# Causal masks of a fused attention kernel: two matmuls into PSUM, or additions by VectorE in place

## The chip, the cores and the metric

The kernel runs on one core of one Trainium2 chip. A core has TensorE (PE in the profile: matmuls; PEld is its weight load), VectorE (DVE), ScalarE (ACT), GpSimd (POOL) and SyncE (SP), each with its own in-order queue, which wait for each other by semaphores. The metric is the device time of one execution in microseconds (us), smaller is better. Three runs of the kernel before took 1605.15 to 1606.68 us, median 1605.58.

## The reference, cut to what matters

Two layers stand one behind the other. The first is a causal attention with 2 x 16 = 32 (batch, head) pairs, 1024 tokens, head width 64, and a two-step graph network that reuses the attention weights; the second is a local attention with a feed-forward network and isn't touched by the change.

```
b, n, _ = x.shape                       # 2, 1024
q = (xn @ Wq) ... * scale ; k = (xn @ Wk) ... ; v = (xn @ Wv) ...
sim = jnp.einsum('bhid,bhjd->bhij', q, k)
mask_value = -jnp.finfo(sim.dtype).max
causal_mask = jnp.triu(jnp.ones((n, n), dtype=bool), k=1)
sim = jnp.where(causal_mask, mask_value, sim)
attn = jax.nn.softmax(sim.astype(jnp.float32), axis=-1)
out = jnp.einsum('bhij,bhjd->bhid', attn, v)
adj = jnp.clip(attn + eye, 0.0, 1.0); deg = jnp.sum(adj, axis=-1, keepdims=True)
feats = v
for l in range(2):
    h = feats @ gnn_w[l] + gnn_b[l]
    h = jnp.einsum('bij,bjd->bid', adj, h) / deg
    feats = gelu(h + feats)
out = out + feats @ lin_w + lin_b
```

## The kernel before, in words

The first part is a loop over t, the 32 pairs of batch and head, in which the stages of neighbouring heads are interleaved: while head t computes its scores, head t+1 computes its row maxima and head t-1 ends its graph steps. Nothing is scheduled automatically. Each engine's order is the order of the calls in its own function (`tensor`, `vector`, the ScalarE function, `gpsimd`, `sync`), written out by hand, and named signals (`p_` counted by PE, `d_` by VectorE, `a_` by ScalarE, `w_` by GpSimd) carry the dependences.

The scores are computed twice. `smax(t, k)` (12 units a head, PSUM banks 0 and 1 in turn, L613) makes a block of 128 queries by up to 512 keys, and VectorE reduces it to row maxima (L1520). `mrow` (L624) transposes the maxima, ScalarE copies them (L1067), and a DMA (L448) lays them down as a 65th row, so that `scores(t, k)` (12 tiles a head, banks 2 and 3 in turn, L641 and L642) gives scores with the maximum already subtracted, keys on the partitions. ScalarE takes two exponentials of each tile (L1077 to a plain fp32 tile `Es`, L1078 to the rounded `Eh`), VectorE takes out the diagonal (L1534, for the tiles on it) and the rounding rest `El` (L1537). `av` (L659 to L661) multiplies by the values, `graph1` (L680), `graph2` (L694, L695, closed by L699) and `graph2b` (L708) are the graph steps, `tailT` and `tail` (L720, L729) the output projection, `proj` and `projv` (L572 to L574, L593 to L595) make queries, keys and values of later heads. ScalarE's `feats` (L1093, L1096) needs another function table than the exponential, so each head has a table load ahead of it and one (1.28 us) ahead of the next head's first exponential.

Of the 12 units and of the 12 tiles 8 each lie on the diagonal. There a third matmul adds the mask: a bf16 identity times a bf16 mask of 128 x 128 (`cmB`, L615 and L644), in the same accumulation group.

A PE matmul that writes bank b waits until the reader of its last content is through: `smax(t, k)` for `d_max` of unit k-2, `scores(t, k)` for `a_eh` of tile k-2. In loops 18 to 29 VectorE also runs `onward` (layer normalization of finished rows, statistics L1448 to L1461 with one step on GpSimd, L1316), in loops 2 to 5 a smaller `normed`; both stand behind `smax(t+1, 5)`.

Of the kernel before, what the change touches and what calls it, by code (L numbers as in the profile page):

```python
# [77 lines left out]
def program(nc, I, OUT):  # L78
    with ExitStack() as ctx:
# [51 lines left out]
        cmB = sb1([P, 2, P], BF16)  # L131
# [102 lines left out]
        maxes = [(t, k) for t in heads for k in (range(NTL) if t == 0 else (0, 1, 2, 3, 4, 5, 6, 7, 8, 9, 11, 10))]  # L234
        hops = [(t, k) for t in heads for k in (0, 2, 1, 3, 4, 5, 7, 9, 6, 8, 10, 11)]
# [39 lines left out]
        d_ident = signal("d_ident", ["R", "B", "cm"])  # L275
# [4 lines left out]
        d_max = signal("d_max", maxes)  # L280
        d_nm = signal("d_nm", heads)
# [234 lines left out]
        def tensor(e):  # L516
# [81 lines left out]
            def smax(t, k):  # L598
# [5 lines left out]
                q.wait_ge(*d_ident["cm"])  # L604
# [21 lines left out]
            def scores(t, k):  # L626
# [118 lines left out]
            for t in range(NH + 2):  # L745
                scores(t, 0)
                if t in (6, 7):
                    turn(t - 4, 6)
                graph2(t - 1, 9)
                scores(t, 1)  # L750
                graph2(t - 1, 6)
                scores(t, 2)
                smax(t + 1, 0)
                smax(t + 1, 1)
                scores(t, 3)
                tailT(t - 2, 0)
# [19 lines left out]
                projv(t + 1, 0)
                projv(t + 1, 1)
                graph2(t - 1, 8)
                scores(t, 6)
                av(t, 2)  # L780
                smax(t + 1, 6)
                scores(t, 7)
                graph2(t - 1, 10)
                smax(t + 1, 7)
                av(t, 3)
                scores(t, 8)
                smax(t + 1, 8)
                av(t, 4)
                smax(t + 1, 9)
# [228 lines left out]
        def scalar(e):  # L1018
# [50 lines left out]
            def scores(t, k):  # L1069
# [4 lines left out]
                q.wait_ge(*p_sc[t, k])  # L1074
# [62 lines left out]
            for t in range(NH + 2):  # L1137
                scores(t, 0)
                if t in (6, 7):
                    turn(t - 4)  # L1140
                scores(t, 1)
                scores(t, 2)
                scores(t, 3)
                if t == 0:
                    linear(1, 6)
# [6 lines left out]
                if t == 0:  # L1152
                    linear(3, 6)
# [768 lines left out]
```

## Time and profile before

| | |
|---|---|
| median of 3 runs | 1605.58 us (1605.15 to 1606.68) |
| the profiled execution, own time | 1606.24 us |
| its span | 1604.5 us |
| PE busy | 1444.8 us, 90% |
| VectorE busy | 1187.4 us, 74% |
| ScalarE busy | 995.6 us, 62% |
| GpSimd busy | 370.2 us, 23% |

Busy time is the time in which at least one instruction of the engine is recorded. A matmul's record includes the time until its last result is in PSUM, in which the next one already streams, so consecutive records of PE overlap; the distance between two starts is what a matmul costs the stream. The same holds, to a smaller degree, for VectorE and ScalarE. "[0.26 <-ACT t L1078]" behind a row means 0.26 us idle ahead of it, ended by that line.

### The profile page before, as it was taken

How to read it: one execution, taken by the hardware profiler on the slowest of the kernel's cores; microseconds unless marked ns; L12 is line 12 of the kernel's file. 1: busy time of each engine (PE TensorE's matmuls, PEld its weight loads, DVE VectorE, ACT ScalarE, POOL GpSimd, SP SyncE). 2: the span in 40 equal slices, each digit the busy share in tenths (PEclk: the TensorE clock that was granted, in tenths of full speed). 3: DMA queues.
4: the chain of work that ended last, by engine and by line, in shares of the span. 5: the costliest groups of instructions: out<-in, count | busy, mean ns of one | idle time of the engine just before them, and what ended most of it. 6: DMA issues, size and time to landing. Idle time of an engine off the chain costs nothing.

```text
span 1604.5 us, 29173 instructions
## 1 busy us (share of the span) xinstructions
PE 1444.8 (90%) x10194; PEld 1109.6 (69%) x10194; DVE 1187.4 (74%) x3247; ACT 995.6 (62%) x2307; POOL 370.2 (23%) x480
## 2 busy tenths in 40 slices
PE   4899999999999999999999999998467899999896
PEld 3577877778777877777777777776245566666664
DVE  4477777777777777777877788774677888788875
ACT  2366666666667666666666666664345767787663
POOL 2022222211122112222222222211322432222221
PEclk8699999999999999999999999998769999999999
DMA  6011111211111111211112111100300100000100
GB/s 162 14 40 41 27 28 30 47 31 27 27 41 40 27 28 31 50 27 28 27 32 49 27 27 28 42 13 20 95 19 15 24 21 18 21 22 20 25 18 20
DMA packets 39067, 53.31 MB, mean 33 GB/s; under 512 B 11742, under 2 KB 21898, under 8 KB 38922
## 3 DMA queue, kind: packets, MB, share of 16 engines
q1 hardware_dynamic: 38922, 51.46, 14.3%
q8 instruction: 81, 1.33, 0.3%
q14 instruction: 64, 0.52, 0.1%
HBM read 8.84 MB, written 1.05 MB: 6 GB/s over the span
## 4 chain that ended last, share of the span: by engine, by line
PE 43%; DVE 25%; issue 13%; ACT 11%; DMA 3%; POOL 3%; SPq 1%; DVEq 0%; POOLq 0%; ACTq 0%
ACT t L1222 5%; DVE t L1520 4%; PE PS L613 4%; PE PS L729 3%; PE PS L708 3%; PE PS L694 3%; DVE t L1537 3%; PE PS L641 3%; DMA t<-t 3%; PE PS L642 2%; PE PS L695 2%; PE PS L661 2%; PE PS L659 2%; PE PS L660 2%; PE PS L680 2%
## 5 line engine op out<-in xcount | busy, mean ns | idle before, releaser
L1077 ACT ACTIVATE t<-PS 128x512 f32<-128x512 f32 (+3 forms) x384 | 188.9, 492 | 149.3 <-PE PS L642 95.3
L1520 DVE TENSOR_REDUCE t<-PS 128x1 f32<-128x512 f32 (+3 forms) x384 | 211.3, 551 | 81.4 <-PE PS L615 56.8
L1537 DVE TENSOR_TENSOR t<-t 128x512 fp32r<-128x512 f32 (+3 forms) x384 | 212.3, 553 | 10.9 <-ACT t L1078 10.8
L1078 ACT ACTIVATE t<-PS 128x512 fp32r<-128x512 f32 (+3 forms) x384 | 188.6, 491 | 0.0
L694 PE MATMUL PS<-t 128*128 128x512 f32 (+3 forms) x384 | 150.2, 391 | 22.1 <-ACT t L1111 21.6
L613 PE MATMUL PS<-t 128*128 128x512 f32 (+3 forms) x384 | 141.4, 392 | 24.5 <-DMA t<-t 12.5
L1222 ACT ACTIVATE t<-PS,t 128x128 f32<-128x128 f32 x256 | 113.2, 463 | 67.0 <-DVE t L1766 67.0
L641 PE MATMUL PS<-t 128*128 128x512 f32 (+3 forms) x384 | 149.8, 390 | 2.7 <-DMA t<-t 2.2
L1408 POOL TENSOR_TENSOR t<-t 128x16 f32<-128x16 f32 x32 | 92.8, 2899 | 240.6 <-DVE t L1722 240.6
L659 PE MATMUL PS<-t 128*66 128x512 f32 (+3 forms) x384 | 138.8, 361 | 0.0
L642 PE MATMUL PS<-t 65*128 65x512 f32 (+3 forms) x384 | 134.4, 350 | 0.0
L660 PE MATMUL PS<-t 128*66 128x512 f32 (+3 forms) x384 | 129.4, 337 | 0.0
L695 PE MATMUL PS<-t 128*128 128x512 f32 (+3 forms) x384 | 129.2, 345 | 0.0
L661 PE MATMUL PS<-t 128*66 128x512 f32 (+3 forms) x384 | 128.4, 338 | 0.0
L1534 DVE SCALAR_TENSOR_TENSOR t<-t 128x128 f32<-128x128 f32 x256 | 72.7, 284 | 57.9 <-ACT t L1077 57.9
L1351 POOL TENSOR_TENSOR t<-t 128x256 f32<-128x256 f32 x64 | 39.2, 613 | 317.3 <-DVE t L1557 317.3
L613 PEld LDWEIGHTS PS<-t 128*128 128x128 f32 x384 | 73.4, 198 | 41.8 <-DVE t L1520 20.2
L1316 POOL TENSOR_TENSOR t<-t 128x2 f32<-128x2 f32 (+1 forms) x42 | 33.8, 804 | 295.8 <-DVE t L1455 295.8
L694 PEld LDWEIGHTS PS<-t 128*128 128x128 f32 x384 | 73.3, 191 | 38.2 <-ACT t L1111 26.1
L641 PEld LDWEIGHTS PS<-t 128*128 128x128 f32 x384 | 75.0, 195 | 20.5 <-ACT t L1078 9.9
L680 PEld LDWEIGHTS PS<-t 66*128 66x128 f32 x512 | 64.6, 190 | 24.2 <-ACT t L1085 18.3
L1111 ACT COPY t<-PS 128x512 f32<-128x512 f32 x64 | 37.4, 585 | 67.6 <-PE PS L699 67.6
(188 smaller groups left out, 3880.5 us busy)
## 6 DMA issues: line engine op xcount, KB each, us to landing
t<-t SPq DMA_DIRECT2D x188, 128.0 KB, 2.3
t<-t SPq DMA_DIRECT2D x64, 256.0 KB, 3.4
t<-in_L_ffn_wqkv SPq DMA_DIRECT2D x2, 768.0 KB, 7.1
t<-in_L_attn_Wv SPq DMA_DIRECT2D x2, 512.0 KB, 7.9
t<-in_c_rot SPq DMA_DIRECT2D x2, 512.0 KB, 5.0
out<-t SPq DMA_DIRECT2D x4, 256.0 KB, 2.3
t<-in_L_ffn_w SPq DMA_DIRECT2D x2, 341.0 KB
t<-in_L_attn_x SPq DMA_DIRECT2D x2, 256.0 KB, 3.2
```

Source lines behind the costliest of these rows:

```text
L613: m = e.matmul(bank(b)[:, 0:hi - lo], Q1[r][:, ib * P:(ib + 1) * P], K1[r][:, lo:hi], start=True, stop=not diag)
L641: e.matmul(b[:, 0:n], K1[r][:, jb * P:(jb + 1) * P], Q1[r][:, i0:i0 + n], start=True, stop=False)
L642: m = e.matmul(b[:, 0:n], K2[r][:, jb * P:(jb + 1) * P], Q2[r][:, i0:i0 + n], start=False, stop=not diag)
L659: e.matmul(dst, VH[r][:, jb, :], Eh[:, o:o + n], start=(jb == 0), stop=False)
L660: e.matmul(dst, VL[r][:, jb, :], Eh[:, o:o + n], start=False, stop=False)
L694: e.matmul(dst, F2[:, jb, :], Eh[:, o:o + n], start=(jb == 0), stop=False)
L695: e.matmul(dst, F2[:, jb, :], El[:, o:o + n], start=False, stop=False).then_inc(p_hop.up((t, k)), 1)
L1077: e.activation(Es[:, k % NS, 0:n], b[:, 0:n], ACT.Exp).then_inc(a_es.up((t, k)), 1)
L1078: e.activation(Eh[:, o:o + n], b[:, 0:n], ACT.Exp).then_inc(a_eh.up((t, k)), 1)
L1222: m = e.activation(E[u][:, n, :], bank(SB + j)[:, c * P:(c + 1) * P], ACT.Exp, bias=nmx[u][:, n:n + 1], scale=sc8[w][:, n:n + 1], accum_ou ...
L1520: e.tensor_reduce(n[:, c, ib:ib + 1], bank(k % 2)[:, 0:hi - lo], AX.X, ALU.max, negate=True).then_inc(d_max.up((t, k)), 1)
L1537: e.tensor_tensor(El[:, o:o + n], Es[:, k % NS, 0:n], f32(Eh[:, o:o + n]), ALU.subtract).then_inc(d_el.up((t, k)), 1)
```

## The change

Both mask matmuls go, with the bf16 mask tile. VectorE adds the fp32 mask `cm` to the 128 columns on the diagonal in place in PSUM: `causal(t, k)` ahead of the reduction in `smax`, `acausal(t, k)` ahead of the exponentials. VectorE's reduction waits for `d_cm`, ScalarE's first exponential of a diagonal tile waits for `d_sm`. The calls of PE, VectorE and ScalarE in the loop stand in another order; GpSimd's and SyncE's are unchanged.

```diff
@@ tensor: smax
-                q.wait_ge(*d_ident["cm"])
                 lo, hi = c * 512, min((ib + 1) * P, (c + 1) * 512)
-                diag = c == ib // 4
-                m = e.matmul(bank(b)[:, 0:hi - lo], Q1[r][:, ib * P:(ib + 1) * P], K1[r][:, lo:hi], start=True, stop=not diag)
-                if diag:
-                    m = e.matmul(bank(b)[:, hi - lo - P:hi - lo], identB[:], cmB[:, 0, :], start=False, stop=True)
-                m.then_inc(p_max.up((t, k)), 1)
+                e.matmul(bank(b)[:, 0:hi - lo], Q1[r][:, ib * P:(ib + 1) * P], K1[r][:, lo:hi], start=True,
+                         stop=True).then_inc(p_max.up((t, k)), 1)
@@ tensor: scores
-                diag = jb >= 4 * c
                 e.matmul(b[:, 0:n], K1[r][:, jb * P:(jb + 1) * P], Q1[r][:, i0:i0 + n], start=True, stop=False)
-                m = e.matmul(b[:, 0:n], K2[r][:, jb * P:(jb + 1) * P], Q2[r][:, i0:i0 + n], start=False, stop=not diag)
-                if diag:
-                    m = e.matmul(b[:, 0:P], identB[:], cmB[:, 1, :], start=False, stop=True)
-                m.then_inc(p_sc.up((t, k)), 1)
+                e.matmul(b[:, 0:n], K2[r][:, jb * P:(jb + 1) * P], Q2[r][:, i0:i0 + n], start=False,
+                         stop=True).then_inc(p_sc.up((t, k)), 1)
@@ ScalarE: scores
                 q.wait_ge(*p_sc[t, k])
+                if jb >= 4 * c:
+                    q.wait_ge(*d_sm[t, k])
                 q.wait_ge(*(d_el[t, k - NS] if k >= NS else d_el[t - 1, k + NTL - NS]))
@@ vector
+            def causal(t, k):
+                if t >= NH:
+                    return
+                ib, c = UNITS[k]
+                o = ib % 4 * P
+                q.wait_ge(ld["cm"], 16)
+                q.wait_ge(*p_max[t, k])
+                s = bank(k % 2)[:, o:o + P]
+                e.tensor_tensor(s, s, cm[:, 0, :], ALU.add).then_inc(d_cm.up((t, k)), 1)
@@ vector: smax
+                if c == ib // 4:
+                    q.wait_ge(*d_cm[t, k])
                 q.wait_ge(*p_max[t, k])
@@ vector
+            def acausal(t, k):
+                if t >= NH:
+                    return
+                q.wait_ge(ld["cm"], 16)
+                q.wait_ge(*p_sc[t, k])
+                s = bank(2 + k % 2)[:, 0:P]
+                e.tensor_tensor(s, s, cm[:, 1, :], ALU.add).then_inc(d_sm.up((t, k)), 1)
@@ vector: the first head's maxima, and the head of the loop
             for k in range(NTL):
+                if UNITS[k][1] == UNITS[k][0] // 4:
+                    causal(0, k)
                 smax(0, k)
             for t in range(NH + 2):
+                acausal(t, 0)
+                acausal(t, 1)
                 scores(t, 0)
...
+                acausal(t, 2)
+                causal(t + 1, 1)
                 smax(t + 1, 0)
-                scores(t, 1)
                 smax(t + 1, 1)
...
```

ScalarE at the turn from one head to the next, before. L1111 is the copy of `hopend`, L1093 and L1096 are `feats(t, 1)`, L1077 and L1078 the exponentials of tiles 0 and 1 of the next head:

```order
L1067 CAST t<-PS 8x128 [waits s_row,p_row]
L1111 COPY t<-PS 128x512 [waits p_g2b,p_hopend]
L1093 ACTIVATE t<-t 128x256 [waits d_pre]
L1096 CAST t<-t 128x4x64 [waits a_ge1]
L1077 ACT_TABLE_LOAD [waits p_hop,d_el]
L1077 ACTIVATE t<-PS 128x512 [waits p_sc]
L1078 ACTIVATE t<-PS 128x512
```

And the same place in the changed kernel, where L1115 is `gelu2`, L1090 and L1093 `feats`, L1074 and L1075 the exponentials:

```order
L1062 CAST t<-PS 8x128 [waits s_row,p_row]
L1108 COPY t<-PS 128x512 [waits p_g2b,p_hopend]
L1115 ACTIVATE t<-t 128x8x64 [waits d_o1,w_p2]
L1090 ACTIVATE t<-t 128x256 [waits d_pre]
L1093 CAST t<-t 128x4x64 [waits a_ge1]
L1074 ACT_TABLE_LOAD [waits d_el,p_hop,d_sm]
L1074 ACTIVATE t<-PS 128x512 [waits p_sc]
L1075 ACTIVATE t<-PS 128x512
```

`gelu2` has moved to this place from ahead of `mrow`'s copy, and the wait for `d_sm`, VectorE's mask on tile 0, stands ahead of the table load; the wait for `p_sc` stands on the exponential behind it, as before.

PE from the first tile of a head (L641 and L642 with a wait for `s_row`) to its third (the wait for `a_eh`), before; L694 and L695 are `graph2` of the head before:

```order
L641 MATMUL PS<-t 128x512 [waits d_low,s_row]
L642 MATMUL PS<-t 128x512
L644 MATMUL PS<-t 128x128
L694 MATMUL PS<-t 128x384 [waits d_f2]
L695 MATMUL PS<-t 128x384
L641 MATMUL PS<-t 128x384 [waits d_low]
L642 MATMUL PS<-t 128x384
L644 MATMUL PS<-t 128x128
L694 MATMUL PS<-t 128x512
L695 MATMUL PS<-t 128x512
L641 MATMUL PS<-t 128x256 [waits a_eh]
```

And in the changed kernel, with L638 and L639 for the tiles, L689 and L690 for `graph2`:

```order
L638 MATMUL PS<-t 128x512 [waits d_low,s_row]
L639 MATMUL PS<-t 128x512
L638 MATMUL PS<-t 128x384 [waits d_low]
L639 MATMUL PS<-t 128x384
L689 MATMUL PS<-t 128x384 [waits d_f2]
L690 MATMUL PS<-t 128x384
L689 MATMUL PS<-t 128x512
L690 MATMUL PS<-t 128x512
L689 MATMUL PS<-t 128x512
L690 MATMUL PS<-t 128x512
L638 MATMUL PS<-t 128x256 [waits a_eh]
```

The second tile stands directly behind the first, and a third call of `graph2` (two matmuls of 512 columns) has come in ahead of the third tile.

VectorE behind `smax(t+1, 5)`, the place where `onward` is put in, before: L1520 is a reduction, L1537 the rest `El`, L1509 and L1510 `projv`.

```order
L1520 TENSOR_REDUCE t<-PS 128x1 [waits p_max] x2
L1537 TENSOR_TENSOR t<-t 128x512 [waits a_eh,a_es]
L1520 TENSOR_REDUCE t<-PS 128x1 [waits p_max]
L1509 TENSOR_TENSOR t<-PS,t 128x4x64 [waits d_pre,a_v]
L1510 TENSOR_TENSOR t<-PS,t 128x256
L1537 TENSOR_TENSOR t<-t 128x512 [waits a_eh,a_es]
```

And in the changed kernel, with L1517 for `causal`, L1541 for `acausal`, L1529 for the reductions, L1554 for `El`, L1506 for `projv`:

```order
L1529 TENSOR_REDUCE t56<-PS 128x1 [waits p_max]
L1517 TENSOR_TENSOR PS<-PS,t4 128x128 [waits p_max]
L1554 TENSOR_TENSOR t58<-t59,t57 128x512 [waits a_eh,a_es]
L1529 TENSOR_REDUCE t56<-PS 128x1 [waits d_cm]
L1554 TENSOR_TENSOR t58<-t59,t57 128x512 [waits a_eh,a_es]
L1541 TENSOR_TENSOR PS<-PS,t4 128x128 [waits p_sc]
L1529 TENSOR_REDUCE t56<-PS 128x1 [waits p_max]
L1506 TENSOR_TENSOR t33<-PS,t31 128x4x64 [waits d_pre,a_v]
```

Unit 7's reduction (the last L1529) now has two masks and two `El` subtractions between it and unit 5's (the first); before, it had unit 6's reduction and one subtraction.

## Rows read from the trace of the kernel before

**Rows 1.** The page: engines' busy time, share of the span, instructions.

```profile
PE 1444.8 (90%) x10194; PEld 1109.6 (69%) x10194; DVE 1187.4 (74%) x3247; ACT 995.6 (62%) x2307; POOL 370.2 (23%) x480
```

**Rows 2.** Four heads: PE, PEld, DVE, ACT, POOL busy (instructions), clock, DMA share, GB/s.

```profile
343.23:473.51 130.28, 126.15 (x833) 101.83 (x832) 96.68 (x281) 85.44 (x185) 27.89 (x48) 1.00 0.16 34
```

**Rows 3.** Timeline, PE: a mark once per head; start us, duration us.

```profile
447.65 0.39 PE L624 MATMUL PS<-t 128*8 128x128 f32 x2
...
609.80 0.39 PE L624 MATMUL PS<-t 128*8 128x128 f32 x2
...
643.22 0.39 PE L624 MATMUL PS<-t 128*8 128x128 f32 x2
...
1040.01 0.38 PE L624 MATMUL PS<-t 128*8 128x128 f32 x2
```

**Rows 4.** Groups by line and shape: busy us, mean ns, idle before.

```profile
L644 PE MATMUL PS<-t 128*128 128x128 bf16 x256 | 59.6, 233 | 0.0
...
L1520 DVE TENSOR_REDUCE t<-PS 128x1 f32<-128x128 f32 x64 | 17.9, 280 | 33.1 <-PE PS L615 32.9
L1534 DVE SCALAR_TENSOR_TENSOR t<-t 128x128 f32<-128x128 f32 x256 | 72.7, 284 | 57.9 <-ACT t L1077 57.9
```

**Rows 5.** Timeline, PE, three masks in the middle of a head.

```profile
498.36 0.39 PE L642 MATMUL PS<-t 65*128 65x512 f32 x1
498.60 0.23 PE L644 MATMUL PS<-t 128*128 128x128 bf16 x1
498.64 0.42 PE L613 MATMUL PS<-t 128*128 128x384 f32 x1
498.90 0.23 PE L615 MATMUL PS<-t 128*128 128x128 bf16 x1
498.94 0.42 PE L659 MATMUL PS<-t 128*66 128x512 f32 x1
499.20 0.40 PE L660 MATMUL PS<-t 128*66 128x512 f32 x1
```

**Rows 6.** Timeline, all engines, from `graph1(t, 1)` to the next head's third tile.

```profile
478.75 1.16 PE L680 MATMUL PS<-t 66*128 66x130 f32 x8
479.95 0.16 DVE L1557 TENSOR_TENSOR t<-PS,t 128x4 f32<-128x4 f32 x1 [0.68 <-PE PS L680]
482.21 0.42 ACT L1093 ACTIVATE t<-t 128x256 f32<-128x256 f32 x1
483.08 1.28 ACT L1077 ACT_TABLE_LOAD   x1
483.81 0.40 PE L641 MATMUL PS<-t 128*128 128x512 f32 x1
484.04 0.40 PE L642 MATMUL PS<-t 65*128 65x512 f32 x1
484.55 0.60 ACT L1077 ACTIVATE t<-PS 128x512 f32<-128x512 f32 x1 [0.18 <-PE PS L644]
485.04 0.59 ACT L1078 ACTIVATE t<-PS 128x512 fp32r<-128x512 f32 x1
...
485.69 0.19 PEld L641 LDWEIGHTS PS<-t 128*128 128x128 f32 x1 [0.26 <-ACT t L1078]
```

**Rows 7.** Timeline, VectorE, middle of a head.

```profile
497.12 0.29 DVE L1520 TENSOR_REDUCE t<-PS 128x1 f32<-128x128 f32 x1 [2.04 <-PE PS L615]
497.33 0.68 DVE L1537 TENSOR_TENSOR t<-t 128x512 fp32r<-128x512 f32 x1
```

**Rows 8.** Waits, four heads with `onward`, 640 to 770 us: total, times, longest.

```profile
PEld PS L613 <- DVE t L1520: 4.5, 8, 0.9
```

**Rows 9.** Waits in four heads without it, 343 to 473 us.

```profile
PEld PS L613 <- DVE t L1520: 1.0, 4, 0.3
```

**Rows 10.** Timeline, VectorE, the first head's reductions.

```profile
35.23 1.02 DVE L1520 TENSOR_REDUCE t<-PS 128x1 f32<-128x512 f32 x2 [7.98 <-PE PS L613]
...
43.79 0.29 DVE L1520 TENSOR_REDUCE t<-PS 128x1 f32<-128x128 f32 x1 [0.37 <-PE PS L615]
```

More of the change, by code:

```diff
@@ L280, in program @@
         d_max = signal("d_max", maxes)
+        d_cm = signal("d_cm", maskings)
+        d_sm = signal("d_sm", [(t, k) for t, k in by_tile if tiles[k][1] >= 4 * tiles[k][0]])
         d_nm = signal("d_nm", heads)
@@ L748, in tensor @@
                     turn(t - 4, 6)
+                scores(t, 1)
                 graph2(t - 1, 9)
-                scores(t, 1)
                 graph2(t - 1, 6)
+                graph2(t - 1, 8)
                 scores(t, 2)
@@ L754, in tensor @@
                 smax(t + 1, 1)
-                scores(t, 3)
+                av(t, 0)
                 tailT(t - 2, 0)
@@ L768, in tensor @@
                     linear(2, 7)
+                scores(t, 4)
+                tail(t - 2, 0)
+                scores(t, 5)
+                av(t, 1)
+                scores(t, 6)
                 smax(t + 1, 4)
@@ L771, in tensor @@
                     linear(3, 6)
-                scores(t, 5)
                 tail(t - 2, 1)
-                av(t, 1)
+                av(t, 2)
+                scores(t, 7)
+                scores(t, 8)
                 smax(t + 1, 5)
+                smax(t + 1, 6)
                 projv(t + 1, 0)
+                av(t, 3)
                 projv(t + 1, 1)
[L778 to L782, printed above, removed]
+                scores(t, 9)
+                smax(t + 1, 7)
+                smax(t + 1, 8)
                 graph2(t - 1, 10)
[L784 to L787, printed above, removed]
+                graph2(t - 1, 11)
+                smax(t + 1, 9)
                 av(t, 4)
-                smax(t + 1, 9)
+                scores(t, 10)
+                scores(t, 11)
                 av(t, 5)
@@ L812, in tensor @@
                 graph2(t, 2)
+                graph2(t, 1)
                 mrow(t + 1)
-                graph2(t, 1)
                 graph2(t, 3)
@@ L1671, in vector @@
                     linear(0, 7)
+                share(t - 1, 1)
+                acausal(t, 3)
+                scores(t, 1)
+                causal(t + 1, 2)
+                scores(t, 2)
                 smax(t + 1, 2)
-                scores(t, 2)
                 scores(t, 3)
+                causal(t + 1, 3)
+                scores(t, 4)
+                smax(t + 1, 3)
                 tail(t - 2, 0)
-                smax(t + 1, 3)
+                smax(t + 1, 4)
                 tail(t - 2, 1)
-                scores(t, 4)
-                smax(t + 1, 4)
-                share(t - 1, 1)
+                scores(t, 5)
+                acausal(t, 8)
                 smax(t + 1, 5)
@@ L1685, in vector @@
                     onward(2 * ((t - 18) % 4), (t - 18) // 4)
+                causal(t + 1, 6)
+                scores(t, 6)
                 smax(t + 1, 6)
-                scores(t, 5)
+                scores(t, 7)
+                acausal(t, 9)
                 smax(t + 1, 7)
                 projv(t + 1, 0)
-                scores(t, 6)
+                causal(t + 1, 8)
                 projv(t + 1, 1)
-                scores(t, 7)
-                smax(t + 1, 8)
+                causal(t + 1, 9)
+                acausal(t, 10)
                 scores(t, 8)
@@ L1697, in vector @@
                     linear(5, 7)
-                smax(t + 1, 9)
+                smax(t + 1, 8)
+                acausal(t, 11)
                 scores(t, 10)
@@ L1701, in vector @@
                 scores(t, 11)
+                smax(t + 1, 9)
+                feats(t, 0)
                 graph2b(t - 1)
-                feats(t, 0)
                 lower(t + 2, 0, 2)
+                causal(t + 1, 11)
+                causal(t + 1, 10)
+                smax(t + 1, 11)
                 lower(t + 2, 1, 3)
-                smax(t + 1, 11)
+                smax(t + 1, 10)
                 share(t, 0)
-                smax(t + 1, 10)
                 graph1(t, 1)
```

53 lines of the change are left out of this document (22 added, 31 removed).

## The prediction, made before the changed kernel ran

> **What bounds the kernel now.** I read the page first: PE is busy 90% of the span, VectorE 74% [rows 1]. A share over the whole span doesn't say what a head costs, so next come windows. In four heads, 343.23 to 473.51 us, PE is busy 126.15 of 130.28 us, VectorE 96.68, ScalarE 85.44, at a granted clock of 1.00, which is 2.4 GHz [rows 2]. Per head (32.57 us) that is 31.5, 24.2 and 21.4 us. PE bounds the loop; VectorE has 8.4 us a head to spare, ScalarE 11.2. The marks that come once a head give 162.15 us for five heads without extra work, 32.43 us each, and 396.79 us for the twelve with `onward`, 33.07 each [rows 3]. So extra VectorE work in one place already costs PE about 0.6 us a head, with VectorE busy only some three quarters: what counts is where a wait lies, not the share. The time in the second part can't change, its code is the same.
>
> **What leaves PE.** 16 mask matmuls a head, 512 in all. Their records are 233 ns long [rows 4], 119 us together, but that is latency. In the stream a mask takes the distance to the next start: 498.60 to 498.64 and 498.90 to 498.94, 0.04 us [rows 5]. It also gives too little cover for the weight load of the matmul behind it: L613 with 384 columns takes 0.26 us to the next start behind a mask, L659 with 512 also 0.26, where L642 needs 0.24 for 512 columns [rows 5], so 384 columns should need 0.18. That is 0.02 to 0.08 more. A matmul behind a wait pays some of it anyway. I take 0.08 us per mask in all, bounds 0.04 and 0.13: 1.3 us a head (0.6 to 2.1), 42 us over 32 heads (20 to 67).
>
> **What comes to VectorE.** 16 additions of 128 columns a head, reading and writing PSUM. No row shows VectorE writing PSUM. Nearest are a reduction of 128 columns from PSUM, 280 ns, and the diagonal operation of 128 columns in SBUF, 284 ns [rows 4]; the next instruction starts 0.21 us behind such a reduction (497.12 to 497.33) [rows 7]. So each costs 0.21 us of the queue, 0.28 us where the next one needs its result. 16 of them are 3.4 to 4.5 us, VectorE goes to 27.6 to 28.7 us a head, and 32.43 less 1.3 would leave it 2.4 to 3.5 us idle. That fits only if it never waits long.
>
> The Trainium skill has a rule against this: "VectorE: DVE Perf Modes", section on the DRAIN, says that the next operation does not start until the pipe is empty. This trace has the next start 0.21 us into a record of 0.29, so the overlap is there; by the rule the additions would take the full 4.5 us a head. The same page, section on the TRN2 errata, gives 58 fixed cycles from SBUF and 120 from PSUM, an estimate of 0.065 us more for each addition, 1.0 us a head; here 280 ns from PSUM and 284 from SBUF show no difference.
>
> **What the wait for the mask does at the turn of the head.** This is the term that decides. Before, ScalarE finishes the gelu and its cast, loads the exponential's table from 483.08 for 1.28 us, and is ready at 484.36, while PE still works on `graph2` and tile 0; tile 0 starts on PE at 483.81, its second matmul at 484.04, the first exponential at 484.55 [rows 6]. The load costs nothing because it hides behind PE's work. In the changed order the wait for `d_sm` stands ahead of the table load, and `p_sc` behind it. So the load can't begin before VectorE has masked tile 0. From the start of tile 0 on PE: second matmul 0.23 later, its record 0.40, about 0.03 to VectorE, 0.28 for the addition, 0.04 to ScalarE, 1.28 table load, 0.49 to the second exponential (484.55 to 485.04) and 0.59 for it, 0.06 back to PE: 3.4 us. Before, this distance was 1.88 us (483.81 to 485.69), of which PE waited 0.26 [rows 6]. The third tile waits for it (same bank as the first). PE's work in between is now tile 0 0.47, tile 1 0.35, and `graph2` with 384, 512 and 512 columns, 0.37 + 0.46 + 0.46: 2.1 us at the spacings of rows 5 (0.23 to 0.24 for 512). The wait is 1.3 us, less the 0.26 of before: +1.05 us a head. Queued behind the waiting tile on PE are `smax(t+1, 0)` and `smax(t+1, 1)`, `av(t, 0)` and all the rest; VectorE meanwhile stands at the diagonal of tile 0, with `acausal(t, 2)` and the causal masks behind it, so it can't use the time. It could be as low as +0.9 if the load's record overlaps the wait a little, or +1.4 if VectorE comes late to the mask.
>
> It may come late: VectorE's chain behind `graph1(t, 1)` began 1.20 us after PE's start of it (478.75 to 479.95, 0.68 us idle before) and reached gelu 2.26 us later [rows 6]. Now PE has `graph1(t, 1)` one `graph2` behind `smax(t+1, 10)`, and VectorE has two masks, two reductions and a `lower` to finish first; I get it 1.0 us later. The table load has slack for that since it waits anyway, and the mask on tile 0 then comes 0.04 late. I put +0.1 (0 to 1.0).
>
> **Other waits in the loop.** Following the two orders with these spacings, PE waits some 0.2 us for the exponentials of tile 6 ahead of tile 8, and 0.35 at `mrow`, for the last maxima; a wait of 0.25 us at `smax(t+1, 10)`, in the 1.0 us over four heads of rows 9, goes. Sum +0.3 (-0.3 to +1.0). The other masks lengthen the way from PE to ScalarE by 0.28 us each, hidden where PE has other work.
>
> A plain head: -1.3 + 1.05 + 0.1 + 0.3 = +0.15 us. 32 heads: +5 us.
>
> **The heads with `onward` and `normed`.** `onward` puts statistics, a step on GpSimd that VectorE waits for, and the normalization behind `smax(t+1, 5)`. Before, VectorE was idle 2.04 us just there [rows 7], which took most of it; what was left shows as PE waiting for the reductions, 4.5 against 1.0 us over four heads [rows 8, 9], about 0.9 a head, and as the 0.64 us by which the period is longer. Now masks and `El` fill this place, I find 0.7 to 1.1 us of slack there instead of 2.0, and PE's `smax(t+1, 9)` waits for unit 7. It costs 0 to 0.9 more a head, 0.5 taken, in 12 + 4 loops: +8 us.
>
> **The start.** The first head's twelve reductions run from 35.23 to 44.08 us with gaps [rows 10]; eight additions there, each needed by the reduction behind it, are 2.2 us, partly in the gaps: +1.5 (0 to 3).
>
> Sum: +5 + 8 + 1.5 = +14.5 us on the profiled execution's own 1606.24 us, 1620.7. That execution is 0.66 us above the median of the runs, so 1605.6 + 14.5 = **1620 us**.
>
> **Rivals.**
> Faster: the wait at the turn is real but takes the place of others, and masks are worth more. At the upper price of a mask, 2.1 us a head, with +1.05 at the turn and nothing else: -1.05 us a head, -34 us, 1572; with 1.7 and the +8 us of `onward`, -13 to -21 us, 1588. For it: PE was 97% busy in these heads, and the new order may remove small exposures that I can't see in rows. Against it: PE's records leave only 1.1 us a head idle (130.28 less 126.15, over four [rows 2]), part of it at `hopend`'s copy, a chain of the same calls in both orders. I take 1588.
> Slower by far: VectorE becomes the bound. If its additions take 0.28 us in the queue, 28.7 us busy, plus waits in its own chains that no order fills (before 8.4 us idle, of which I count 4.4 at the turn, in the two `graph1` chains and at `feats`, and 1.3 more now), a head is 34.4 us, +2 us, +63 us: 1669. It decides once busy time and chain waits exceed 32.4. A middle case, 33.2 us a head, is 1630 to 1645. Against it: the spacing of 0.21.
> No difference: the two large terms, -1.3 and +1.15, cancel and `onward` costs nothing more: 1603 to 1609.
> The clock: it is 1.00 in the loop [rows 2]; with one more wait of 1.3 us in 32 PE would still be busy over nine tenths of a head, so I give a lower clock no case of its own.
>
> **How the numbers follow.** My forecast 0.5 (its own range 1609 to 1636), faster 0.27, VectorE as the bound 0.13, no difference 0.10. A change of under 0.2%, 3.2 us, can't be told from none. Slower 0.63, same 0.10, faster 0.27. The range reaches down to the chosen faster case with its own spread, 1583, and up into the middle case of VectorE, 1643.
>
> **What would show it.** A table load at the head's turn that starts some 0.7 us after tile 0's last matmul and not right behind the cast; PE idle 1.0 to 1.4 us ahead of the third tile, put down to ScalarE's second exponential; L615 and L644 gone; VectorE near 28 us a head at 0.21 us per addition; a period of about 32.6 us in plain heads and 33.7 with `onward`. I am wrong if the load starts right behind the cast as before (then -1.0 us a head more, about 1587), or if plain heads are shorter than 32 us with the wait in place (masks mis-sized), or if VectorE has no idle time left (the third case).

## The result, and the profile after

Five runs of the changed kernel have a median of 1619.63 us (1614.08 to 1621.98), five of the kernel before 1606.68 us (1605.15 to 1608.01). The ratio is 1.0076 with a 95% interval of 1.0054 to 1.0097: slower, by 13 us. The profiled execution took 1619.94 us, span 1618.1.

The page of the changed kernel, its busy line, in the columns of [rows 1]:

```profile
PE 1413.6 (87%) x9682; PEld 1109.4 (69%) x9682; DVE 1279.4 (79%) x3758; ACT 992.3 (61%) x2307; POOL 375.5 (23%) x480
```

512 matmuls are gone and PE is busy 31 us less; VectorE is busy 92 us more and the span 13.6 us longer. Windows of four plain heads (columns as in [rows 2]) and of the first two with `onward`:

```profile
324.84:450.58 125.74, 118.23 (x770) 99.85 (x769) 107.88 (x346) 84.78 (x184) 28.29 (x48) 1.00 0.16 35
...
639.22:674.15 34.93, 31.48 (x193) 25.93 (x192) 28.93 (x95) 21.33 (x46) 8.15 (x13) 0.95 0.15 31
674.15:708.87 34.72, 31.40 (x193) 26.10 (x192) 29.01 (x95) 21.33 (x46) 8.15 (x13) 0.95 0.15 32
```

A plain head takes 31.43 us instead of the 32.57 of [rows 2]: the change makes the loop's body faster. VectorE is busy 26.97 us a head, 2.8 more than before. In the heads with `onward` PE is busy as long as before the change with fewer matmuls, at a granted clock of 0.95. The marks once per head, PE, at the places of [rows 3]:

```profile
450.58 0.39 PE L622 MATMUL PS<-t 128*8 128x128 f32 x2
...
607.82 0.39 PE L622 MATMUL PS<-t 128*8 128x128 f32 x2
...
639.22 0.39 PE L622 MATMUL PS<-t 128*8 128x128 f32 x2
...
1052.34 0.38 PE L622 MATMUL PS<-t 128*8 128x128 f32 x2
```

Five plain heads: 157.24 us, 31.45 each, against 32.43. (Over all twelve of loops 6 to 17 the means are 31.44 and 32.71, since some heads of the kernel before take 33 us.) The twelve with `onward`: 413.12, 34.43 each, against 33.07. From all marks of both kernels, the difference by stretch of the loop:

| loops | after less before, us |
|---|---|
| up to the first mark | +0.15 |
| loop 0 | +9.70 (53.72 against 44.02) |
| loop 1 | 0.0 |
| 2 to 5, with `normed` | +1.45 |
| 6 to 17, plain | -15.3 |
| 18 to 29, with `onward` | +16.3 |
| loop 30, and behind it | +1.3 |
| sum | +13.6 |

The turn of the head, all engines, as [rows 6] showed it before:

```profile
516.68 0.41 ACT L1093 CAST t<-t 128x256 fp32r<-128x256 f32 x1
516.95 0.40 PE L638 MATMUL PS<-t 128*128 128x512 f32 x1
517.18 0.40 PE L639 MATMUL PS<-t 65*128 65x512 f32 x1
517.62 0.65 DVE L1541 TENSOR_TENSOR PS<-PS,t 128x128 f32<-128x128 f32 x2
517.98 1.28 ACT L1074 ACT_TABLE_LOAD   x1 [0.90 <-DVE PS L1541]
519.28 0.60 ACT L1074 ACTIVATE t<-PS 128x512 f32<-128x512 f32 x1
519.77 0.59 ACT L1075 ACTIVATE t<-PS 128x512 fp32r<-128x512 f32 x1
...
520.41 0.38 PE L638 MATMUL PS<-t 128*128 128x256 f32 x1 [1.19 <-ACT t L1075]
```

The cast ends at 517.09, and the load starts 0.90 us later, when VectorE's first addition is through. From the start of tile 0 to the third tile: 3.46 us, and PE idles 1.19 of it.

What the additions and their neighbours take, groups by shape (busy us, mean ns, idle before), beside [rows 4]:

```profile
L1541 DVE TENSOR_TENSOR PS<-PS,t 128x128 f32<-128x128 f32 x256 | 75.2, 294 | 43.2 <-PE PS L639 41.8
L1551 DVE SCALAR_TENSOR_TENSOR t<-t 128x128 f32<-128x128 f32 x256 | 72.3, 283 | 52.5 <-ACT t L1074 52.4
...
L1517 DVE TENSOR_TENSOR PS<-PS,t 128x128 f32<-128x128 f32 x256 | 71.3, 289 | 1.7 <-PE PS L613 1.2
```

The heads with `onward`, timeline of VectorE, PE and ScalarE at the place of [rows 7] and [rows 8]:

```profile
692.24 0.82 DVE L1458 TENSOR_SCALAR t<-t 128x128 f32<-128x128 f32 x2 [0.82 <-POOL t L1313]
...
693.46 0.28 DVE L1517 TENSOR_TENSOR PS<-PS,t 128x128 f32<-128x128 f32 x1
693.66 0.68 DVE L1554 TENSOR_TENSOR t<-t 128x512 fp32r<-128x512 f32 x1
694.26 0.28 DVE L1529 TENSOR_REDUCE t<-PS 128x1 f32<-128x128 f32 x1
...
694.60 0.45 PE L613 MATMUL PS<-t 128*128 128x384 f32 x1 [1.44 <-DVE t L1529]
...
695.53 1.05 PE L694 MATMUL PS<-t 128*128 128x128 f32 x4
...
696.91 0.63 PE L654 MATMUL PS<-t 128*66 128x512 f32 x1
...
697.34 0.63 PE L655 MATMUL PS<-t 128*66 128x512 f32 x1
...
698.71 0.40 PE L654 MATMUL PS<-t 128*66 128x512 f32 x1
```

VectorE first waits 0.82 us for GpSimd in the middle of `onward`, then does the normalization, and only then the mask and the reduction on which PE waits: 1.44 us. In the waits of these four heads (639 to 779 us) PE's longest at L613 is 1.5 and its weight load's 1.8; before, from 640 to 770 us, they were 0.8 and 0.9 [rows 8]. Behind it four small matmuls of L694 take 1.05 us (0.61 at full clock), and the 512-column ones stand 0.43 us apart (696.91 to 697.34) instead of 0.23: PE is at 1.2 GHz for some three us, and back by 698.71. That is the 0.95 of the window. The clock falls in this way in loops 18 to 25, all eight; in loops 26 to 29 the wait is 0.7 to 1.1 us, the clock stays at 1.00, and a head takes 32.8 to 33.1.

### The profile page after: what moved, and what is told of

It is laid out like the page before. It is cut to its first block and busy times, and to the rows that moved or that the text cites. A ratio compares the mean times of both kernels' runs of the same rounds, so it can differ in the third digit from the quotient of the medians.

```text
span 1618.1 us, 28788 instructions
## 1 busy us (share of the span) xinstructions
PE 1413.6 (87%) x9682; PEld 1109.4 (69%) x9682; DVE 1279.4 (79%) x3758; ACT 992.3 (61%) x2307; POOL 375.5 (23%) x480
## 3 DMA queue, kind: packets, MB, share of 16 engines
HBM read 8.84 MB, written 1.05 MB: 6 GB/s over the span
## 5 line engine op out<-in xcount | busy, mean ns | idle before, releaser
L1074 ACT ACTIVATE t<-PS 128x512 f32<-128x512 f32 (+3 forms) x384 | 192.2, 500 | 181.9 <-PE PS L639 91.9
L1554 DVE TENSOR_TENSOR t<-t 128x512 fp32r<-128x512 f32 (+3 forms) x384 | 212.2, 553 | 10.8 <-ACT t L1075 10.8
L1529 DVE TENSOR_REDUCE t<-PS 128x1 f32<-128x512 f32 (+3 forms) x384 | 207.9, 548 | 9.2 <-PE PS L613 8.5
L1075 ACT ACTIVATE t<-PS 128x512 fp32r<-128x512 f32 (+3 forms) x384 | 191.7, 499 | 0.1
L638 PE MATMUL PS<-t 128*128 128x512 f32 (+3 forms) x384 | 143.7, 377 | 42.0 <-ACT t L1075 39.7
L689 PE MATMUL PS<-t 128*128 128x512 f32 (+3 forms) x384 | 138.7, 368 | 24.1 <-ACT t L1108 21.6
L613 PE MATMUL PS<-t 128*128 128x512 f32 (+3 forms) x384 | 124.7, 385 | 31.0 <-DVE t L1529 22.1
L654 PE MATMUL PS<-t 128*66 128x512 f32 (+3 forms) x384 | 139.4, 363 | 0.3 <-issue 0.3
L639 PE MATMUL PS<-t 65*128 65x512 f32 (+3 forms) x384 | 134.2, 358 | 0.0
L655 PE MATMUL PS<-t 128*66 128x512 f32 (+3 forms) x384 | 134.2, 349 | 0.0
L656 PE MATMUL PS<-t 128*66 128x512 f32 (+3 forms) x384 | 131.9, 347 | 0.0
L690 PE MATMUL PS<-t 128*128 128x512 f32 (+3 forms) x384 | 131.6, 352 | 0.0
L638 PEld LDWEIGHTS PS<-t 128*128 128x128 f32 x384 | 76.5, 199 | 71.5 <-ACT t L1075 57.3
L1541 DVE TENSOR_TENSOR PS<-PS,t 128x128 f32<-128x128 f32 x256 | 75.2, 294 | 43.2 <-PE PS L639 41.8
L613 PEld LDWEIGHTS PS<-t 128*128 128x128 f32 x384 | 71.8, 199 | 52.2 <-DVE t L1529 35.4
L1313 POOL TENSOR_TENSOR t<-t 128x2 f32<-128x2 f32 (+1 forms) x42 | 33.8, 804 | 309.7 <-DVE t L1452 309.7
L689 PEld LDWEIGHTS PS<-t 128*128 128x128 f32 x384 | 73.9, 192 | 41.6 <-ACT t L1108 26.2
L639 PEld LDWEIGHTS PS<-t 65*128 65x128 f32 x384 | 76.6, 199 | 5.9
```

Of the source, the lines that this page charges most:

```text
L654: e.matmul(dst, VH[r][:, jb, :], Eh[:, o:o + n], start=(jb == 0), stop=False)
L655: e.matmul(dst, VL[r][:, jb, :], Eh[:, o:o + n], start=False, stop=False)
L656: m = e.matmul(dst, VH[r][:, jb, :], El[:, o:o + n], start=False, stop=(jb == 4 * c + 3))
L689: e.matmul(dst, F2[:, jb, :], Eh[:, o:o + n], start=(jb == 0), stop=False)
L1074: e.activation(Es[:, k % NS, 0:n], b[:, 0:n], ACT.Exp).then_inc(a_es.up((t, k)), 1)
L1075: e.activation(Eh[:, o:o + n], b[:, 0:n], ACT.Exp).then_inc(a_eh.up((t, k)), 1)
```

## The experiments

Each was timed against the kernel before on the same chip (1607.03 us beside e1 to e4, 1610.03 beside e5, e6, e7 and e9, 1608.19 beside e8). Periods are the distances of PE's marks in the profiled execution, typical plain heads first, then the mean over the twelve heads with `onward`, then loop 0 with its mean granted clock.

| kernel | median us | ratio (95%) | plain | `onward` | loop 0 | its clock |
|---|---|---|---|---|---|---|
| before | 1606.68 | 1 | 32.43 | 33.07 | 44.0 | 0.75 |
| changed | 1619.63 | 1.0076 (1.0054 to 1.0097) | 31.43 | 34.43 | 53.7 | 0.63 |
| e1_load_free | 1588.57 | 0.9894 (0.9862 to 0.9927) | 30.34 | 33.4 | 58.5 | 0.53 |
| e2_order_only | 1593.28 | 0.9933 (0.9910 to 0.9956) | 31.54 | 32.7 | 49.9 | 0.67 |
| e3_masks_only | 1862.51 | 1.1611 (1.1555 to 1.1667) | 40.99 | 41.5 | 45.5 | 0.73 |
| e4_before_nomask | 1591.25 | 0.9914 (0.9881 to 0.9947) | 31.66 | 32.7 | 40.5 | 0.80 |
| e5_new_order_no_masks | 1563.57 | 0.9713 (0.9682 to 0.9743) | 30.34 | 32.1 | 49.7 | 0.63 |
| e6_loop0_old | 1585.50 | 0.9847 (0.9812 to 0.9881) | 30.37 | 33.5 | 45.5 | 0.73 |
| e9_linear_moved | 1588.66 | 0.9870 (0.9830 to 0.9910) | 30.35 | 33.4 | 49.6 | 0.63 |
| e7_split | 1579.64 | 0.9811 (0.9777 to 0.9844) | 30.37 | 32.8 | 50.1 | 0.65 |
| e8_split_late | 1593.50 | 0.9907 (0.9884 to 0.9930) | 30.36 | 33.6 | 49.7 | 0.64 |

**The table load set free.** In the changed kernel, one wait of ScalarE is dropped that another covers: VectorE's addition itself waits for PE, so `p_sc` isn't needed on a diagonal tile. Of the waits that the source puts ahead of the exponential, the first one written stands on the exponential itself and the others ahead of the table load: before and in the changed kernel the first is `p_sc`, with `d_sm` among the others. With `p_sc` gone `d_sm` is the first, and the load has only `d_el` and `p_hop`, which it had before. (Writing `d_sm` ahead of `p_sc` should do the same; no run tried it.)

```diff
-                q.wait_ge(*p_sc[t, k])
-                if jb >= 4 * c:
-                    q.wait_ge(*d_sm[t, k])
+                q.wait_ge(*(d_sm if jb >= 4 * c else p_sc)[t, k])
```

> The changed kernel, but on the diagonal tiles ScalarE waits for VectorE's mask alone and no longer for PE's tile as well (the mask already waits for it). The wait for the mask then stands on the exponential, and the table load ahead of it waits for nothing new. Theory A (the table load behind the mask costs PE 1.2 us in each of 31 turns, and everything behind it runs as before that): the load starts right behind the cast, PE waits 0 to 0.3 us ahead of the third tile, plain heads go from 31.43 to 30.3-30.6 us, the time to 1583-1592 us. Rival B (VectorE's chains bind the loop and the load's wait only covers for them): the wait goes elsewhere, plain heads stay at 31.2-31.5, 1610-1618 us.

The turn of a plain head, timeline:

```profile
478.79 0.41 ACT L1091 CAST t<-t 128x256 fp32r<-128x256 f32 x1
479.22 1.28 ACT L1072 ACT_TABLE_LOAD   x1
479.26 0.40 PE L638 MATMUL PS<-t 128*128 128x512 f32 x1
...
479.93 0.65 DVE L1539 TENSOR_TENSOR PS<-PS,t 128x128 f32<-128x128 f32 x2 [0.20 <-PE PS L639]
480.51 0.60 ACT L1072 ACTIVATE t<-PS 128x512 f32<-128x512 f32 x1
...
481.65 0.39 PE L638 MATMUL PS<-t 128*128 128x256 f32 x1
```

The load starts 0.02 us behind the cast and covers tile 0 and its mask; the third tile comes 2.39 us behind the first instead of 3.46. That 1.07 us is the difference in the period, 31.43 to 30.34, within 0.02. What held the load was the place of a wait, not the addition. Period and time (1588.57 us) came as theory A had them. In both kernels the first exponential starts 1.29 to 1.30 us after its load does. The Trainium skill, "ScalarE: Activation LUTs", section "What ACT_TABLE_LOAD costs", adds a drain of about 1.38 us to each load's 1.28; here neither cast to load nor load to exponential shows one.

**The order alone.** The kernel before, with its mask matmuls, and the changed kernel's order of calls on PE, VectorE and ScalarE.

```diff
 (tensor, vector, ScalarE: the loop over t)
-  the calls in the order of before
+  the calls in the order of the changed kernel, without causal and acausal
```

> The kernel before (masks as matmuls on PE) with the new order of calls on PE, VectorE and ScalarE, without the two mask calls of VectorE. Theory A (a mask on PE is worth some 0.1 us, and the new order is by itself no worse than the old): about the time before, 1595-1610 us, plain heads 31.9-32.4 us, since no table load waits for a mask. Rival B (the new order fits only a loop whose masks lie on VectorE): slower than before, over 1612 us.

It came out faster than either theory had it: 31.54 us a plain head and 1593.28 us.

**The masks alone.** The other half: the old order, with each addition put directly ahead of the reduction, or one call of `scores` ahead of the exponentials, that needs it.

```diff
+                acausal(t, 3)
                 scores(t, 2)
...
+                causal(t + 1, 3)
                 smax(t + 1, 3)
```

> The other half: masks added by VectorE, the old order of calls, each mask directly ahead of the reduction it serves or one call ahead of the exponential. Theory A: the turn costs 0.4 us more than in the changed kernel (one graph2 less of cover ahead of the third tile, 1.6 us of waiting), and masks stand ahead of VectorE work that PE waits for in the middle of a head; plain heads 32.5-33.5 us, 1640-1670 us. Rival B (the search of the order bought nothing): within 5 us of the changed kernel, 1615-1625 us.

Both theories missed by far: 41 us a plain head, 1862.51 us. More on it below.

**No masks, in either order.** The kernel before without L615 and L644 (e4), and the changed kernel without any `causal` and `acausal` and their waits (e5). In both the scores aren't masked.

```diff
e4, smax and scores on PE
-                if diag:
-                    m = e.matmul(bank(b)[:, hi - lo - P:hi - lo], identB[:], cmB[:, 0, :], start=False, stop=True)
e5, vector and ScalarE
-                acausal(t, 0)
...
-                    q.wait_ge(*d_sm[t, k])
```

> The kernel before without its 512 mask matmuls and with no mask in their place (the scores are not masked; nothing else is left out): the price of a mask on PE by itself. As the prediction put it, 0.08 us per mask, 1.3 us a head: 1562-1568 us. If the whole gain of a plain head in the changed kernel (31.43 against 32.43, with a new wait of 1.2 us in it) is the masks' price, it is 0.13 us per mask, 2.1 us a head: 1538-1545 us.

> The changed kernel's order of calls with no masks at all: no mask matmuls on PE and no additions on VectorE (the scores are not masked; nothing else is left out). Beside the order alone with PE masks (plain heads 31.54 us, 1593 us) it gives the price of PE's masks in the new order; beside the changed kernel with the table load set free (30.34 us, 1589 us) it gives the price of VectorE's 16 additions. Theory A (PE's masks cost 0.07-0.1 us each where nothing else binds; VectorE's additions are nearly free in plain heads but not in the first loop and with onward): plain heads 30.0-30.4 us, onward heads 31-31.6 us, first loop 44-50 us, 1560-1575 us. Rival (in the new order too the masks of PE cover waits, 0.03-0.05 us each): plain heads 30.8-31.1 us.

e4, at 1591.25 us, lies 23 us above the range for 0.08 us a mask; e5 came as theory A had it, but for its heads with `onward`, 32.1 us.

One plain head of each, windows, columns as in [rows 2]. The order alone:

```profile
475.96:507.50 31.54, 30.86 (x210) 25.29 (x209) 23.89 (x72) 20.87 (x46) 7.05 (x12) 1.00 0.16 34
```

The new order without masks, and below it a head with `onward`:

```profile
582.97:613.31 30.34, 29.54 (x194) 24.95 (x193) 23.87 (x71) 21.08 (x46) 7.07 (x12) 1.00 0.17 36
...
678.69:710.59 31.90, 30.00 (x193) 24.97 (x192) 25.99 (x79) 21.20 (x46) 8.06 (x13) 1.00 0.16 34
```

And the load set free, with all additions on VectorE:

```profile
475.89:506.22 30.33, 29.53 (x193) 24.94 (x192) 26.79 (x86) 21.17 (x46) 7.07 (x12) 1.00 0.17 35
```

So a plain head comes apart in four steps: 32.43, by the order alone -0.89 to 31.54, by the masks leaving PE -1.20 to 30.34, by 16 additions on VectorE nothing (30.33, though VectorE is busy 2.9 us more), by the held table load +1.10 to 31.43. A mask was worth 0.075 us of PE in the new order, 0.048 in the old (32.43 to 31.66 in e4): in the old order PE's idle time grows from 0.95 to 1.2 us a head and takes back part of it. These are the typical heads. Over all twelve plain heads the means are 32.71, 31.73, 30.54, 30.62 and 31.44, so the held load is worth 0.8 us there and not 1.1: with the load free some heads are longer than 30.3, one of them by a wait of 1.0 us for a DMA.

The masks alone cost 8.5 us a head, 32.43 to 41. Part of that is the clock. One plain head ran at 1.00, the one below; it took 38.52 us, where the five from loop 13 on took 41 at 0.92. So some 2.5 us are the clock and 6 the waits.

```profile
329.76:368.28 38.52, 31.71 (x196) 25.52 (x197) 29.43 (x87) 22.01 (x47) 6.95 (x12) 1.00 0.13 28
```

In the window of four heads, 550 to 712 us (waits: total, times, longest):

```profile
ACT t L1074 <- PE PS L639: 34.5, 19, 3.3
...
PEld PS L638 <- ACT t L1075: 15.0, 11, 2.1
...
DVE PS L1517 <- PE PS L613: 13.2, 8, 2.0
...
PEld PS L724 <- ACT t L1122: 9.2, 4, 2.3
```

PE waits for ScalarE's exponentials, ScalarE for PE's scores, and VectorE stands at a mask until PE has made its unit. I read it as in-order queues that block each other in turn; which wait starts the ring I haven't separated. The turn alone is as expected, 1.67 us of PE's idle time ahead of the third tile in most heads; what the expectation lacked is the rest. The price holds for my placing of the additions, one call early at most; it isn't the price of additions as such, since the changed order hides them all in the plain heads.

**Loop 0.** Two versions on top of e1: all three engines' calls of loop 0 in the old order (e6), or only VectorE's `linear(5, 7)` moved from ahead of `smax(t+1, 8)` to behind `scores(t, 10)` (e9).

```diff
e6, in each of the three loops
+                if t == 0:
+                    scores(t, 0)
...
+                    continue
e9, vector
-                if t == 0:
-                    linear(5, 7)
                 smax(t + 1, 8)
                 acausal(t, 11)
                 scores(t, 10)
+                if t == 0:
+                    linear(5, 7)
```

> The changed kernel with the table load set free, and in the first loop alone (t = 0) the old order of calls on PE, VectorE and ScalarE, with VectorE's masks put in as in the run of masks only, whose first loop took 45.5 us. Theory A (the first loop is lengthened by the order that the calls have there, VectorE waiting for the linear layer's matmuls with a mask behind it): first loop 45-47 us instead of 54-58, the rest as with the load set free, 1574-1580 us. Rival (the long first loop comes from the three heads' warm-up at the low clock and VectorE's masks anyway): 52 us or more, 1585-1592 us.

> The changed kernel with the table load set free, and one call of VectorE moved: linear(5, 7), which runs in the first loop only, stands behind scores(0, 10) instead of ahead of smax(1, 8), so that the mask on tile 11 no longer waits behind it. Theory A: ScalarE's 7 us wait for that mask goes, PE's 2.3 us wait ahead of graph1(0, 0) and the fall to the low clock behind it too; the first loop 48-53 us instead of 58 (54 in the changed kernel), 1578-1586 us. Rival (the first loop's length is set by the low clock up to 80 us, by waits at 66 us): 56-58 us, no change beyond 2 us.

Loop 0 of the changed kernel, timeline (L560 is a `linear` of PE, L1481 its copy by VectorE, L675 `graph1`):

```profile
81.40 3.73 PE L560 MATMUL PS<-t 64*128 64x128 f32 x32
85.17 0.29 DVE L1481 COPY t<-PS 128x128 f32<-128x128 f32 x1 [4.55 <-PE PS L560]
...
86.94 0.28 ACT L1074 ACTIVATE t<-PS 128x128 f32<-128x128 f32 x1 [7.07 <-DVE PS L1541]
...
88.30 2.07 PE L675 MATMUL PS<-t 66*128 66x130 f32 x8 [2.34 <-ACT t L1033]
```

And with the call moved (e9):

```profile
80.34 0.28 ACT L1072 ACTIVATE t<-PS 128x128 f32<-128x128 f32 x1 [1.50 <-DVE PS L1539]
...
84.70 1.06 PE L675 MATMUL PS<-t 66*128 66x130 f32 x8
```

In the changed kernel VectorE stands at `linear(5, 7)`, which waits for PE, with the mask of tile 11 queued behind it; ScalarE waits 7.07 us for that mask, and PE's `graph1` 2.34 us for ScalarE. The same eight matmuls then take 2.07 us instead of 1.06, so PE runs at 1.2 GHz there. With the call moved the chain is gone, the loop 0 of e9's trace is 49.6 us as expected, but e9's time, 1588.66 us, is above its range (1578 to 1586) and the same as e1's 1588.57. So no gain in time is shown for the move.

The traces of loop 0 can't be compared one by one, because of the clock. Length times mean granted clock, an estimate of what the loop would take at full clock, is 31.0 to 33.8 us in all eleven kernels: 33.0 before, 33.8 in the changed kernel, 31.0 in e1, 31.2 in e9, 33.2 in e6. So the longer time at 1.2 GHz can account for up to 9 of the 9.7 us (less, as far as PE waits in it). In e1 PE is at 1.2 GHz from before loop 0 until 98.4 us, and the 32 matmuls of L560 take 7.03 us there instead of 3.73; in e9 the clock has risen at 79.3 us, in e5, without any additions, at 78.7. e6 and e7 have identical instructions in loop 0. They run within 0.04 us of each other for 21 us behind the first mark, then e6's clock rises (64.6 us) and e7's only at 75.1, and the loops end 4.6 us apart. What makes the clock rise later in the changed kernel isn't shown: e2 and e5, in the new order without additions, have 49.9 and 49.7 us, and e7 and e8, in the old order with them, 50.1 and 49.7. So e6's 45.5 us, within its range, doesn't show that the order is the cause; its time of 1585.50 us is 5 us above its range.

**The normalization cut in two.** On top of e6, statistics stay behind `smax(t+1, 5)`; what follows GpSimd's step moves behind `smax(t+1, 7)` (e7), and `normed` is cut in the same way. A second version has the halves behind `smax(t+1, 7)` and `scores(t, 9)` (e8).

```diff
                 smax(t + 1, 5)
-                    onward(2 * ((t - 18) % 4), (t - 18) // 4)
+                    onward(2 * ((t - 18) % 4), (t - 18) // 4, 0)
...
                 smax(t + 1, 7)
+                    onward(2 * ((t - 18) % 4), (t - 18) // 4, 1)
```

> As the kernel with the old order in the first loop, and in loops 2 to 5 and 18 to 29 the layer normalization on VectorE cut in two: statistics behind smax(t+1, 5) as before, the normalization itself behind smax(t+1, 7), so that VectorE doesn't stand waiting 0.8 us for GpSimd and unit 7's maxima, which PE waits for, come ahead of the second half. Theory A (in these heads PE's wait of 1.4 us at smax(t+1, 9), and the half clock that follows a wait of this length, make the 3.5 us over a plain head): the wait goes and the clock stays at 1.00, heads with onward 31.0-31.8 us instead of 33.9, 1545-1560 us. Rival B (VectorE is full in these heads, at 29 us busy, so the wait only moves): 33-34 us, within 6 us of the kernel without the cut.

> As the kernel with the normalization cut in two, but both halves later on VectorE: the statistics behind smax(t+1, 7), where before they stood behind smax(t+1, 5), and the normalization behind scores(t, 9). Theory A (PE's wait in these heads comes only from unit 7's maxima standing behind the statistics): nothing stands ahead of unit 7 any more, heads with onward 31.2-32.2 us instead of 32.6, clock 1.00, 1568-1578 us. Rival B (VectorE, 29.8 us busy of 32.6 there, is the bound of these heads): 32.4-33.0 us, within 4 us of 1579.6.

Two heads of e6, undivided:

```profile
684.58:717.01 32.43, 30.03 (x193) 24.98 (x192) 28.83 (x95) 21.29 (x46) 8.18 (x13) 1.00 0.16 33
650.55:684.58 34.03, 31.63 (x194) 25.97 (x193) 29.13 (x95) 21.27 (x46) 8.16 (x13) 0.95 0.15 32
```

PE in these two heads, timeline:

```profile
669.91 0.44 PE L613 MATMUL PS<-t 128*128 128x384 f32 x1 [1.45 <-DVE t L1642]
...
673.37 0.63 PE L654 MATMUL PS<-t 128*66 128x512 f32 x1
...
703.95 0.45 PE L613 MATMUL PS<-t 128*128 128x384 f32 x1 [1.45 <-DVE t L1642]
...
707.55 0.39 PE L654 MATMUL PS<-t 128*66 128x512 f32 x1
```

One of e7:

```profile
652.93:685.52 32.59, 30.40 (x193) 24.90 (x193) 29.84 (x95) 21.06 (x46) 7.69 (x13) 1.00 0.16 34
```

One of e8, a window and three rows of its timeline:

```profile
658.14:691.68 33.54, 30.32 (x193) 24.87 (x193) 29.96 (x95) 21.04 (x46) 7.88 (x13) 1.00 0.15 33
```

```profile
682.82 0.29 DVE L1656 TENSOR_TENSOR PS<-PS,t 128x128 f32<-128x128 f32 x1
...
683.14 0.28 ACT L1147 ACTIVATE t<-PS 128x128 f32<-128x128 f32 x1 [2.84 <-DVE PS L1656]
...
684.69 2.00 PE L703 MATMUL PS<-t 128*128 128x64 f32 x16 [1.06 <-ACT t L1181]
```

The same wait of 1.45 us stands in both heads of e6, at the same place. Behind one of them the clock falls (0.63 us records 3.5 us later) and the head costs 34.03 us; behind the other it stays at 2.4 GHz, and it costs 32.43. So the wait doesn't decide alone. Split, all twelve heads of e7 stay at 1.00, and the mean falls from 33.5 to 32.8. A split head at full clock isn't shorter than an undivided one at full clock (32.59 against 32.43): the split pays through the clock. The wait has only moved, as Rival B said: in each of these heads PE waits some 1.1 us at `graph2` near the head's end (683.17 us in the one above, L689, ended by VectorE's L1730). So e7 missed its range, 32.8 us against 31.0 to 31.8 and 1579.64 us against 1545 to 1560. e7 has the lowest ratio of the kernels here that mask the scores, 1.9% below the kernel before, though its interval overlaps e6's.

e8 missed too. Its clock is 1.00 in ten of the twelve heads, and typical ones are 0.95 us longer than e7's: the second half now stands ahead of the mask of tile 11, the last of the head, which comes 24.68 us behind PE's mark instead of 23.72, and ScalarE waits 2.84 us for it instead of 1.50. ScalarE's copy for `hopend` (L1181) stands behind that exponential, and PE's `graph2b` (L703) now waits 1.06 us for the copy, where e7 records no idle time of PE. So the later place lies on a chain that ends at PE.

## Why the prediction was right, and where it wasn't

The time, 1620 us against 1619.63, and the sign were right. Two steps were right with their sizes; several others were wrong in ways that cancelled, and that the total came out within a microsecond is luck. The prediction had named a sign of being wrong, plain heads shorter than 32 us with the wait in place, and it came: 31.43. The reason given there, masks mis-sized, isn't the one; it is the order of calls.

- **The wait at the turn: right, with its size.** Forecast 3.4 us from tile 0 to the third tile, a PE wait of 1.3, +1.05 us a head; measured 3.46, 1.19, and +1.10 when the load alone is set free (e1). It was read from the order of waits and from the durations of [rows 6]. The case named for a load right behind the cast, about 1587 us, is what e1 measured, 1588.57, with the other errors in it too. The further +0.1 for a late mask isn't seen: VectorE starts it at 517.62, 0.04 us behind tile 0's last record.
- **A mask on PE: right.** Forecast 0.08 us, 1.3 a head, from the 0.04 us spacing plus the lost cover of the next weight load [rows 5]; measured 1.20 in the new order (e2 to e5), though only 0.77 in the old (e4).
- **An addition on VectorE: right that it's hidden, high in size.** Forecast 3.4 to 4.5 us a head in the queue; busy time rose by 2.8 (26.97 less 24.17), and the period not at all (e5 to e1). VectorE as the bound, at 0.13, didn't come. The next instruction starts 0.20 us into a record of 0.28 behind an addition (693.46 to 693.66), as it did before; the additions' 289 and 294 ns stand beside 283 in SBUF. Neither the full drain nor the 62 extra cycles from PSUM, by the Trainium skill's "VectorE: DVE Perf Modes" (sections on the DRAIN and on the TRN2 errata), shows here. The section on the DRAIN itself adds, and the prediction left out, that a next operation which is not held starts earlier; that agrees.
- **"Other waits in the loop", +0.3 us a head: wrong.** The new order by itself is worth -0.89 (e2). I had bounded it at -0.3, since PE's records left only 1.1 us idle. But in the new order PE's busy time fell too, from 31.5 to 30.86 with the same matmuls, and its idle time only from 0.94 to 0.68. The distances from one start to the next changed at many places, by under a quarter us in any group of like matmuls, so the step can't be put down to one wait. With it right, a plain head would have been -1.0 and not +0.15. The sum had +1.8 us over loops 6 to 17, measured were -15.3, and the faster rival had its mechanism in these heads.
- **`onward` and `normed`, +8 us: wrong in size.** I added 0.5 us a head to a plain head of +0.15. Measured, the twelve heads with `onward` are 1.36 us longer each than before, while a plain head is 1.0 shorter: 2.4 us of extra cost. The place was right, PE's unit 9 waiting for unit 7's reduction. Two things failed. The wait was sized too small: at full clock such a head is 0.7 us longer than a plain one before (33.14 against 32.43), 1.2 in the new order alone (e2), 1.6 without masks in it (e5) and 2.1 with the additions (e1 and e6, 32.43 against 30.33), so 1.4 more and not 0.5, and 0.9 of it comes without the additions, which I had named as the cause together with `El`. And "I give a lower clock no case of its own": the 1.44 us wait is followed, in eight of these twelve heads, by a time at 1.2 GHz, worth 1.6 us between e6's two heads.
- **The start: wrong place.** The first twelve reductions cost +0.15, not +1.5. Loop 0, which I counted as a plain head, was 9.7 us longer, and by the estimate above the time at 1.2 GHz (39.5 us of the loop, 22.2 before) can account for up to 9 of it. A wait behind `linear(5, 7)` that the order of calls shows, and that I hadn't looked for, stands in it too; why the clock rose later stays open.

So +9.7 in loop 0 and +17.7 in the heads with layer normalization stood against -15.3 in the plain ones. A single number close to the truth isn't evidence for the sum's terms; e1 and e2 are.

## What to carry to other kernels

Look at what stands between a wait and the instruction that needs it: a table load queued behind a wait lies on the path with its 1.28 us, here 1.1 us a head, and dropping one redundant wait turned 0.8% slower into 1.1% faster. When a cost moves to an engine with time to spare, search the order again, since the same additions cost a plain head nothing in one order and 8.5 us in another; and read the stretches that run once or differ (the first loop, the loops with extra work) as carefully as the typical one. Before a wait of more than a microsecond is accepted on PE, ask what the clock does behind it; and look at the clock before two traces of a stretch near the start are compared.

## What the runs showed of the hardware that I hadn't expected

PE's granted clock fell to 1.2 GHz within some 2 us of a single wait of 1.44 us, in a head in which PE was otherwise nine tenths busy, and stayed there some three us. With the identical wait it did so in one head of e6 and not in the next; what tells them apart I haven't found. Over loops 18 to 25, by the size of PE's wait at this place, it fell in 9 of 9 heads with 1.54 to 1.56 us (e1, e6, e9), in 19 of 23 with 1.40 to 1.46 (the changed kernel, e1, e6, e9), in 2 of 16 with 1.06 to 1.14 (e4, e5), and in none of 16 with 0.78 to 0.91 (before, e2). In loops 2 to 5 and 26 to 29 of the changed kernel, e1, e6 and e9 it fell in 4 of 32, with 0.74 to 1.09. The 1.19 us wait at the turn, between full stretches, left the plain heads at 1.00. In e8 PE is idle 3.2 of 33.54 us, in pieces of at most 1.13, and ten of twelve heads kept 1.00. One of the two at 0.95 took 33.56 us: PE's 1.13 us wait for VectorE near the head's end is gone there, so where VectorE's chain sets the pace the lower clock can cost next to nothing.
